# A graph, attention and expert layer: edge preparation moved into the sweep over the rows, and one exact piece of 128 edges for four target nodes

## The reference, cut to what matters

```
deg  = segment_sum(ones, edge_dst)            # 6250 degrees
dinv = deg ** -0.5
norm = dinv[edge_src] * dinv[edge_dst]
h    = x @ init_w                              # "opening rows"
root = x @ root_w
for t in range(3):
    h = segment_sum(h[edge_src] * norm, edge_dst) + root + b
    h = relu(h)                                # next layer starts from h @ w
# beside it: layer norm of the rows, keys and values of 4 heads,
# each normalised per head, and their 64x64 product summed over all nodes
```

## Time and profile before

| what | value |
|---|---|
| time, median of 3 runs | 3887.31 us (3881.83 to 3890.51) |
| the profiled execution's own time | 3850.21 us |
| its span, granted clock | 3848.3 us, 0.965 |
| PE busy | 3540.3 us (92%), 18289 matmuls |
| DVE busy | 1363.4 us (35%) |
| ACT busy | 739.9 us (19%) |
| group matmuls L1019, L1023 | 2 x 784, mean 342 and 344 ns |
| sums L1034 | 2744, mean 357 ns |
| `place` rows L900 | 1568, mean 314 ns |

### The profile page before, as it was taken

The page is one execution under the profiler, slowest core; times in us unless marked ns, Lnnn a source line. Parts: engine busy times, 40 slices in busy tenths (PEclk is TensorE's granted clock), DMA queues, the critical chain, the costliest instruction groups (busy, mean ns, idle before and its releaser), DMA issues. The chain is left out here.

```text
span 3848.3 us, 51302 instructions
## 1 busy us (share of the span) xinstructions
PE 3540.3 (92%) x18289; PEld 2013.8 (52%) x18290; DVE 1363.4 (35%) x4621; ACT 739.9 (19%) x1516; POOL 239.8 (6%) x255
## 2 busy tenths in 40 slices
PE   3898999999999699999989999999999998757999
PEld 2565455555545355555545555555555554535776
DVE  4445777767674111111111111211112002553444
ACT  0354444444442000000000000000000000432333
POOL 1000000000000000000000000000000000362333
PEclk9998999999999899999999999999999999878999
DMA  6121213131323799999964444898888995326775
GB/s 166 42 71 43 125 67 142 76 142 67 142 95 161 249 317 327 307 321 318 318 201 145 151 155 145 313 296 286 282 286 281 304 304 164 121 105 213 248 238 196
DMA packets 260290, 762.79 MB, mean 198 GB/s; under 512 B 25570, under 2 KB 176410, under 8 KB 258108
## 3 DMA queue, kind: packets, MB, share of 16 engines
q1 hardware_dynamic: 165360, 618.13, 47.0%
q10 hardware_dynamic: 83484, 115.15, 11.2%
q0 software_dynamic: 11312, 27.75, 2.0%
HBM read 533.28 MB, written 240.32 MB: 201 GB/s over the span
## 5 line engine op out<-in xcount | busy, mean ns | idle before, releaser
L1316 PE MATMUL acc<-ring,split 128*128 128x448 f16 x5488 | 1045.7, 353 | 27.6 <-DMA ring<-adj_d 27.6
L1316 PEld LDWEIGHTS acc<-ring,split 128*128 128x128 f16 x5488 | 537.6, 98 | 526.4 <-issue 31.5
L1316 PE MATMUL acc<-ring,other 128*128 128x448 f16 x4116 | 784.8, 353 | 0.0
L1034 PE MATMUL first_sum<-stage,other 128*128 128x448 f16 x2744 | 735.4, 357 | 2.5 <-DVE split L913 2.5
L1316 PEld LDWEIGHTS acc<-ring,other 128*128 128x128 f16 x4116 | 403.2, 98 | 378.4 <-issue 8.1
L1367 DVE TENSOR_TENSOR tmp<-acc,dinv_b 128x448 f32<-128x448 f32 x98 | 60.9, 622 | 1294.7 <-PE acc L1316 1294.7
L854 ACT ACTIVATE stage<-group_ps 128x392 f16<-128x392 f32 x784 | 383.1, 498 | 475.5 <-PE group_ps L1023 475.0
L900 DVE TENSOR_SCALAR place<-iota_col,rel 128x392 f16<-128x392 f16 x1568 | 427.5, 314 | 0.0
L1034 PEld LDWEIGHTS first_sum<-stage,other 128*128 128x128 f16 x2744 | 271.3, 99 | 225.9 <-issue 12.8
L1019 PE MATMUL group_ps<-place,lanes 128*128 128x392 f16 x784 | 268.2, 342 | 61.5 <-DVE place L900 48.6
L897 DVE TENSOR_TENSOR lanes<-iota_two,lane_two 128x256 f16<-128x256 f16 x784 | 224.6, 286 | 150.0 <-PE group_ps L1023 142.3
(11 more groups left out here) (331 smaller groups left out, 2596.6 us busy)
## 6 DMA issues: line engine op xcount, KB each, us to landing
ring<-adj_d SPq DMA_DIRECT2D x490, 784.0 KB, 4.3
adj_d<-stage SPq DMA_DIRECT2D x14, 5488.0 KB, 17.9
row_d<-blank ACTq DMA_DIRECT2D x20, 3340.5 KB, 58.0
slot_weights<-pack_d SPq DMA_DIRECT2D x42, 898.0 KB, 5.2
part_d<-blank ACTq DMA_DIRECT2D x10, 3340.5 KB, 59.6
slot_rows<-row_d SPq DMA_DIRECT2D x42, 393.0 KB, 5.9
rin<-root_d SPq DMA_DIRECT2D x28, 448.0 KB, 8.1
slot_base<-row_d SPq DMA_DIRECT2D x21, 393.0 KB, 5.8
```

Source lines behind the costliest of these rows:

```text
L1034: m = mm(acc[k][:, 0:WIN], other[:, h, half, k * P:(k + 1) * P], stage[:, b, h, :], start=(h == 0 and half == 0), stop=(h == TILES - 1 and ...
L1316: m = nc.tensor.matmul(acc[b][k][:, :], src[:, h, part, k * P:(k + 1) * P], ring[:, i, r, :], start=(h == 0 and part == 0), stop=(h == TIL ...
```

## The change

The two blocks become one, and the barrier stands behind it. The load of x comes in three parts (7, 14 and 28 tiles), and the sweep begins when the first part's scales are known. `LAG` grows from 12 to 40, so there are 89 steps. The edge work is cut into functions that DVE runs at given steps. Runs are integers that hold dst and src in one word; they start every 16 edges and are 128 long. Two gathers fetch 256 edges near a group's start; DVE counts in them where the group's nodes begin (nine columns), and from that computes two exact starts, one for each four nodes, which two further gathers fetch. So each piece of 128 edges belongs to four nodes, `place` has 196 columns, and the two matmuls of a group write one half of the bank each. The flag now also covers an order test of dst and pieces that don't fit. The key pieces:

```diff
+Q4 = COLS // 2
+STEP = 16
+CODE = 13
-            LAG = 12
+            LAG = 40
+            PARTS = ((0, SUB), (SUB, 3 * SUB), (3 * SUB, TILES))
+            RUN_AT, TURN_AT, DEG_AT = 10, 26, 34
 # SP
-                    for rows, flat in ((dst_i, a["dst"]), (src_i, a["src"])):
+                    sp.dma_start(dst_i[...]); sp.dma_start(prev_i[1:FULL + 1, :], ...[:, ROW - 2:ROW])
+                    sp.wait_ge(e_code, 1)
+                    sp.dma_start(lin_d.rearrange("(p x) -> p x", p=P), code_i).then_inc(e_lin, 16)
+                    sp.wait_ge(e_lin, 16)
+                    sp.dma_start(runs_d[:, :], bass.AP(lin_d.tensor, 0, [[STEP, STARTS], [1, P]])).then_inc(e_runs, 16)
+                    sp.dma_start(xin..., bass.AP(lin_d.tensor, 0, [[HALF, P], [HALF * P, XB], [1, P]])).then_inc(x_in, 16)
+                    (then w_root, w_init, b_one: w_in1)
 # POOL
+                    pool.wait_ge(e_runs, 16)
+                    pool.wait_ge(e_idx, 2)
+                    for q in range(PAIRS):
+                        for h in range(2):
+                            nc.gpsimd.indirect_dma_start(near[:, q, h * P:(h + 1) * P], None, runs_d[:, :], ...)
+                    pool.wait_ge(e_start, 1)
+                    (the same for far[:, q, s, :] from start)
 # ACT
+                    act.wait_ge(e_pad, 4)
+                    (src, src's last row)
+                    for part, (lo, hi) in enumerate(PARTS):
+                        act.dma_start(x_all[:, lo:hi, :], ...).then_inc(n_in[part], 16)
+                    act.dma_start(x_all[0:LAST, TILES - 1, :], ...).then_inc(n_in[2], 16)
+                    (copies of the turned wk and wv; x_roots(0); then the steps)
 # DVE
+                    dve.wait_ge(e_in, 48)
+                    (prev_f, lasts)
+                    for i in range(HC):
+                        nc.vector.tensor_scalar(below[:, i, :], eights[:, :], lasts[:, i:i + 1], None, ALU.is_gt).then_inc(e_below, 1)
+                    coded()
+                    dve.wait_ge(n_in[0], 16)
+                    measured(*PARTS[0]); scattered(0); centred(); scales(0)
                     normed(0)
                     normed(1)
+                    first_runs()
                     for j in range(STEPS):
                         if j + 2 < TILES:
                             normed(j + 2)
+                        j == 1: measured(7 to 20)   j == 2: scattered(1)   j == 3: scales(1), tables()
+                        j == 4: ordered()   j == 8: measured(21 to 34)   j == 9: measured(35 to 48), scattered(2)
+                        j == 10: scales(2), near_shifted()   j == 11: near_relative(), column(0)
+                        j == 12: column(4), starts()   j == 13 to 19: one column each   j == 20: flags()
+                        j == 21: split_codes()   22: lanes_known()   23: rows_known()   24: keys_known()
+                        j == 26: verdict()   28: extents()   29: extents_halved()
+                        j == 34: degrees()   36: inverse_roots()   38: dinv_out()
                         if 1 <= j <= TILES:
                             reduced(j - 1)
+                    def column(k):
+                        e.then(nc.vector.tensor_scalar(hit[:, :, :], near_rel[:, :, :], k - 0.5, None, ALU.is_lt))
+                        e.then(nc.vector.tensor_reduce(cum[:, :, k], hit[:, :, :], X, ALU.add))
 # PE, in the steps
+                        if j == RUN_AT + 11: flags_turned()
+                        if 0 <= j - TURN_AT - 1 < PAIRS: runs_turned(j - TURN_AT - 1)
+                        if j == DEG_AT: degrees()
 # the row windows
-                        nc.vector.tensor_scalar(place[:, 2 * u % RING + s, :], iota_col[:, :],
+                        nc.vector.tensor_scalar(place[:, 2 * u % RING + s, :], iota_col[:, 0:Q4],
-                    mm(group_ps[u % BANKS][:, :], lanes[:, u % 4, :, 0], place[:, 2 * u % RING, :], start=True, stop=False, ...)
+                    mm(group_ps[u % BANKS][:, 0:Q4], lanes[:, u % 4, :, 0], place[:, 2 * u % RING, :], start=True, stop=True, ...)
-                    mm(group_ps[u % BANKS][:, :], lanes[:, u % 4, :, 1], place[:, 2 * u % RING + 1, :], start=False, stop=True,
+                    return mm(group_ps[u % BANKS][:, Q4:COLS], lanes[:, u % 4, :, 1], place[:, 2 * u % RING + 1, :], start=True, stop=True,
```

More of the change, by code:

```diff
@@ L237, in front @@
+            counts = tmp("counts", [PG, PAIRS])
+            bound_i = tmp("bound_i", [PG, PAIRS], I32)
+            most = tmp("most", [PG, 2, PAIRS])
+            peak = tmp("peak", [PG, 2])
+            cum = tmp("cum", [PG, PAIRS, CUMS])
             deg = tmp("deg", [PG, PAIRS, G])
@@ L491, in front @@
[L491 to L504 removed]
+            below_words = tmp("below", [P, HC * GROUPS // 2])
@@ new lines, in front @@
+            below = below_words[:, :].bitcast(F16).rearrange("p (i g) -> p i g", i=HC)
+            later = Carve(below_words[:, :])
+            runs = later.take(2, PAIRS, 2 * P)[0:PG].rearrange("g n q (s e) -> g n q s e", s=2)
+            tile_i = later.take(PAIRS * 2 * P, dt=I32)[0:PG]
+            later.at = 0
+            x_tile, x_lane, x_key_f = (later.take(RUNS) for _ in range(3))
+            scratch.at = 0
+            near = scratch.take(PAIRS, REACH, dt=I32)[0:PG]
+            far = near.rearrange("g q (s e) -> g q s e", s=2)
@@ new lines, in _, with split_codes @@
+                    flat = far.rearrange("g q s e -> g (q s e)")
+                    key, lane = (runs[:, n, :, :, :].rearrange("g q s e -> g (q s e)") for n in range(2))
+                    def split_codes():
+                        for q in range(PAIRS):
+                            dve.wait_ge(e_got[q], 32)
+                        e.done(nc.vector.tensor_scalar(tile_i, flat, 7, TILE_MASK, ALU.logical_shift_right, ALU.bitwise_and))
+                        e.then(nc.vector.tensor_scalar(lane_i, flat, P - 1, None, ALU.bitwise_and))
@@ new lines, in lanes_known, with rows_known @@
+                    def lanes_known():
+                        e.done(nc.vector.tensor_copy(lane, lane_i))
+                        e.then(nc.vector.tensor_scalar(flat, flat, CODE, None, ALU.logical_shift_right))
+                    def rows_known():
+                        for q in range(PAIRS):
+                            for s, base in enumerate((g_base, g_base_two)):
+                                e.done(nc.vector.tensor_scalar(runs[:, 0, q, s, :], far[:, q, s, :], base[:, q:q + 1], None, ALU.subtract))
+                        e.settle()
```

767 lines of the change are left out of this document (421 added, 346 removed).

## The result

The kernel after takes 3732.22 us (median of 4 runs, 3727.27 to 3736.48), the kernel before 3884.57 in the same comparison (4 runs, 3877.31 to 3890.51): a ratio of 0.961, 95% interval 0.9593 to 0.9627. That is 152 us less. The forecast was 3778 with a range from 3735 to 3838. The sign was right, and so was the mechanism in the main, but for what holds ScalarE at the start.

What follows compares the result with a forecast made beforehand. Edge preparation was taken as bound by latencies, sweep and windows by TensorE. Group matmuls -82, window border -9, first window -5 and front -13 sum to -109 us, carried to a median of 3778 us, range 3735 to 3838.

Steps and rivals of the forecast that it cites:

- Group matmuls (-82): Thirteen windows: each half-width group matmul falls from 0.163 to 0.098 us, 624 groups, -82 us (bounds 69 and 101).
- Window border (-9): Eight groups at each window's border: about three paced by VectorE, five by TensorE, 0.7 us a window, -9 us in 13.
- First window (-5): First row window: 56 groups paced by VectorE's narrower rows, 6 us less, part lost to stalls, -5 us (bounds 2 and 8).
- Start (-62): Front of the sweep: ScalarE's issue ends at 51 us, first product at 58.6 instead of 120.67, -62 us (bounds 50 and 69).
- the forecast's chain (1.3, 1.2, 2.6, 1.0, 1.5): Between ScalarE's last issue and the first product: table load, copies, centring, scales, and time until the product, in us.
- LAG (+6): Sweep with LAG 40: 28 steps fall by 0.91 us and 28 opening rows are added at 1.13, +6 us.
- VectorE, transposes, flags, w_root, end (+28 +6 +5 +2 +1.5): Added to the sweep, in us: uncovered VectorE work, TensorE transposes, flags with branch, wait for root weights, semaphores and barrier.
- The push of 28 us: Sweep: 74 us of VectorE work against 46 of cover in 24 steps; the other 28 delay TensorE (bounds 12 and 45).
- first rival: Sweep start and steps: ScalarE free near 44 us, VectorE finds more slack, front -41 us, median 3750; chance 12%.
- Carrying to the median: Whole kernel: -109 us on the profiled 3850.2 carried in proportion to the median 3887.3, as -110, giving 3778.
- the overlap works: Same as the first rival: lateness made up in free steps of the sweep, front -41 us, median 3750; chance 12%.
- The slower rival, the clock falling in the sweep: Sweep and window borders: TensorE falls to 1.2 GHz in gaps, +144 us against -109, median 3922; chance 4%.

Runs made afterwards that it cites:

- w98: Kernel after, each group matmul multiplying only 98 of its 196 columns; 13 windows 666.1 us against 709.0 in the kernel after.
- rows392: Kernel after, VectorE writing place rows 392 wide as before while TensorE still reads 196; 13 windows 716.8 us against 709.0.
- split: Kernel after, dst and src loads cut into partitions 0 to 111 and 112 to 117; x issued at 22.2 us instead of 38.4, sweep began 16.2 us earlier.
- lag40: Kernel before with LAG 40 instead of 12 and nothing else; sweep 226.4 us against 220.1.
- wfirst: Kernel after, root and init weights and bias loaded ahead of the codes in SP's queue; sweep 251.5 us, first group at 298.9.
- nofar_wf: wfirst without the second set of 14 gathers; sweep 251.4 us against 253.3 with them on that chip.
- ring16: Kernel after, ring of 16 rows instead of 8, closing of the old window at group 5 instead of 1; 13 windows 668.7 us against 709.0.

## Why the prediction was wrong in size

The four stages came out 47 us better than the forecast's terms: 18 by the price of the group matmul, 12.7 by the start, 13.9 by the sweep and 2.5 by the first window. All four misses lie on one side.

*Group matmuls (-82).* The mis-sized step is the price of a 196-column matmul, taken at 0.098 us from one-column matmuls. It measured 0.083: 624 x 2 x (0.163 - 0.083) = 100 us. The bounds, 0.082 to 0.108, held it, the middle did not. In the earlier trace rows nothing but loads follow each other; here two products of 448 columns stand between one group matmul and the next. w98 shows that half the columns would be covered too. The doubt about going below the price of the load was groundless for this order of matmuls. The prediction's premise that a load must hide under the very matmul before it is too strict as well: in w98 a sum, with weights of its own, starts 0.04 us after a 98-column matmul.

*Window border (-9).* 109.1 - 100 = 9.1 is left for it, so the size was right. The split was not: rows392 puts 7.8 on VectorE, where the forecast had 13 x 3 x 0.11 = 4.3.

*First window (-5).* 4.2 by the rows (rows392). The rest of the 7.5 lies within what two runs of the same window differ by, and is open.

*Start (-62).* 58.6 was forecast, 45.95 came. The step that failed is the end of ScalarE's issue, taken at 51 as 45.7 and a third of the run table's 17 us, with bounds of 44 and 63. It was 38.4, outside them, and the run table was issued at 38.43, so the two never met. What holds the queue was named in the prediction as the rule of the Trainium skill (DMA: Bandwidth & Descriptors, "How many engines (k)"), and weighed only as a reason to be slower. split shows that the loads over 118 partitions set this start. Why the issue ended 7 us sooner than in the kernel before is not shown; no run changes the loads of that kernel. From 38.4 on the forecast's chain (1.3, 1.2, 2.6, 1.0, 1.5) gives 46.0, as measured.

*LAG (+6).* +6.4 alone (lag40). Right.

*VectorE, transposes, flags, w_root, end (+28 +6 +5 +2 +1.5).* Together 28.2 instead of 42.5. In wfirst VectorE's +28 measures 20.9 (steps 7 to 23), the transposes' +6 3.2. The flags' +5 hardly shows: 3.49 us in step 20, 3.27 in step 34 with the register load and the branch, 3.38 in step 36. The push of 28 us was worked out as if the free steps 5 to 7 could not make up for the loaded ones ahead of them. They do: steps 1 to 6 run at 3.22 to 3.23 us. The prediction had named this under its first rival. The slack of 1.9 us a step was not too small, rather too large: by it a column costs 0.8, and 1.27 was measured, a slack of 1.4. So the lower total is not a lower price of a column. w_root was forecast at 2. It is gone in wfirst, and the step that waits for it took 0.7 to 6.9 us over 3.22 elsewhere, in part by the clock.

*Carrying to the median.* The profiled 3850.2 and the median 3884 to 3887 are two kinds of chip and not two sizes of the change. In proportion or as it stands, the difference was 1 us; it did no harm.

*Rivals.* One rival pointed the right way: "the overlap works" had ScalarE free near 44 and more slack on VectorE, front -41. The measured -40.1 matches by some luck, since ScalarE was free at 38.4 and the sweep gave less than that rival had. It kept the matmul's price and so stopped at 3750. The true time needed that rival and the lower bound of the matmul at once. Each had some chance, and a range that ends at 3735 gave their meeting nearly none. The slower rival, the clock falling in the sweep, did not come: 0.99 in the stage, with single steps at 1.2 GHz.

## What to carry to other kernels

The price of a short matmul depends on what stands ahead of it: take it from a row with the same neighbours, and where there is none, let the forecast sit at the columns if a long product stands between any two short ones. Two loads over 118 partitions, first in both queues, starved this start, also of the loads queued behind them; look at the DMA share of the first 20 us, and try such a load cut at a multiple of 16. When work moves into a loop with slack, sum it against every later step that can absorb it, and look at which transfers arrive at a time that the loop does not set: a faster loop only waits longer for them.

## What the runs showed of the hardware that was not expected

- A 128-column load of f16 weights costs nothing between products of 448 columns: 98-column matmuls take 0.04 us of TensorE's time there. By the formula of the Trainium skill (TensorE: Matmul & The Clock Gate, "LDWEIGHTS (loading the stationary operand)") such a load takes 107 ns. The load rows of w98 show 0.10 us, and its matmuls show that this is hidden and not added.
- Two loads over 118 partitions, each first in its queue, held down all that followed: 109 GB/s over 12:16 us, and 348 with the same bytes in 112 and 6 partitions. With both on SP's queue and x on ScalarE's, as in the kernel before, it was 282.
- POOL's indirect gathers can hold ScalarE up 5 to 10 us, and VectorE 0.6 to 8.1, until 2 to 4 us after the last of them has begun, on chips where the kernel before takes 3885 us and more (nine runs of nine), and not where it takes 3850 (six of six without the wait). That it is the gathers is shown (nofar_wf); how they do it, and what differs between the chips, is open. The same chips are slower in one unchanged stage with gathers (TensorE busy 265 us in 400 instead of 301, and 303 in ring16 on a chip of the faster kind); the cause is open.
